# Front attention heads in pairs on the row halves of the array, constants set by DVE, and a new order of segments

## The chip, the cores and the metric

The kernel runs on one NeuronCore of a Trainium2 chip, as one launch. The metric is device time in microseconds (us): 547.35 us is the median of three runs (545.98 to 549.2).

The core has five instruction streams that run side by side and wait for one another through semaphores: PE (TensorE, the matrix engine; its weight loads are listed apart as PEld), DVE (VectorE), ACT (ScalarE), POOL (GpSimd) and SP (SyncE, which here issues every DMA). Each stream executes strictly in the order in which it was written. A place where one stream waits therefore holds up all that stands behind it in that stream.

## The reference

Eight sequences of 256 tokens by 128 features pass four layers, each with a layernorm ahead and a residual add behind:

```python
x = x + attn_a(layernorm(x))   # 16 heads of 8, rotary, causal over all 256 tokens
x = x + ffn(layernorm(x))      # gate, up, down; 352 wide
x = x + attn_b(layernorm(x))   # 16 heads of 8, RMS norm of q and k, causal in groups of 32 tokens
x = x + ffn(layernorm(x))      # the same weights again

def attn_a(x):
    q, k, v = heads(x @ Wq.T), heads(x @ Wk.T), heads(x @ Wv.T)
    q, k = q * cos + rotate(q) * sin, k * cos + rotate(k) * sin
    scores = einsum('bhqd,bhkd->bhqk', q, k) * 8 ** -0.5 + causal_mask
    return merge(softmax(scores) @ v) @ Wo.T

def fp4_linear(x, w):          # x and w are rounded to FP4 in blocks of 16 first
    return einsum('bsk,nk->bsn', fp4(x), fp4(w))

def ffn(x):
    return fp4_linear(silu(fp4_linear(x, w_gate)) * fp4_linear(x, w_up), w_down)
```

## The kernel before, in words

**Stages.** A batch is one sequence, held as two tiles of 128 tokens. Per batch there are four stages: front attention (`attn_a`), FFN a, local attention (`attn_b`), FFN b. Batches don't depend on one another; the stages of one batch do. Ahead of everything stand a setup (constants, masks, the attention weights transposed by PE) and the FP4 rounding of the FFN weights, a chain of wide operations on DVE called `weights` (L1162 to L1189), whose result PE transposes (L681 to L689).

**Front attention.** `front1` normalises the batch (moments on DVE, the root on POOL, the centring L1202 on DVE), transposes it, forms q, k and v on PE (L726, L729), applies the rotation (L1243, L1244) and splits q and k into three bf16 parts each, of which products are formed for nearly f32 accuracy. SP writes the parts to DRAM (`scatter`, L608) and reads them back stacked (`fetch`, L619): head by head 8 features by 6 part products, which is 48 rows. The even heads stand on partitions 0 to 47, the odd heads on 64 to 111. In `Kf` a pair of heads shares one column block, one head on each half. In `Qf` every head has a column block of its own, with the 64 rows of the other half zero, so that a matmul over all 128 rows adds nothing from the neighbour. `front2` makes the scores twice. First (L746 to L750) query by key, of which DVE takes each row's maximum (L1252); the negated maxima are split in three, transposed, and written by DMA into three further rows of `Qf` (`max_rows`, L626), where `Kf` has ones. Then (L765 to L769) key by query with the maximum subtracted, of which ACT takes the exponential (L963); PE multiplies by V (L780). V has a column of ones beside its 8 columns, which yields the softmax denominators. Since the three rows must be zero in the first pass, SP copies `zrows` into them ahead of each fetch (L639). The second pass goes round three PSUM banks (`ring`), so PE may start a pair only when the exponential of the first head of the pair before is done (L763).

**Local attention.** It has the same form, but `Ql` and `Kl` hold pairs on both halves and its matmuls address one half each (`rows`, L828; L847). The block of scores starts with a mask matmul over all 128 rows (L822, L845); the product with V (L858) uses 32 columns of the array at a time.

**Waits at the start.** PE and ACT go past the setup only when `ones_ready` is set, at the end of POOL's memsets (L1040 to L1056). DVE waits for the first DMAs and casts the masks (L1154 to L1160).

**Order.** `TIMES` gives every segment of every stage and batch a position for each engine, and `weave` writes each engine's stream in that order. `FFN_TURNS` fixes in what sequence the two FFNs use banks 6 and 7. Nothing is scheduled at run time.

Of the kernel before, what the change touches and what calls it, by code (L numbers as in the profile page):

```python
# [70 lines left out]
14  # L71
# [52 lines left out]
70 72 77
105 106 114
156 159 165
206 208 214
264 267 272
316 318 323
356 358 360  # L130
387 388 392""",
    "pe.local2": """
# [9 lines left out]
40 42 45 54 57 59 66
74 75 79 88 90 91 95
109 111 115 127 130 142 147
161 163 166 183 188 190 195
210 215 220 243 245 247 248
265 269 271 294 297 301 303
315 320 325 342 344 346 348
357 359 361 379 381 383 384""",
    "pe.ffn_b2": """  # L150
172 174 179 223 226 229 231
254 255 259 275 278 279 284
307 308 311 332 334 337 340
350 352 354 364 366 368 370
372 374 377 389 390 391 393
395 397 400 409 411 412 414
# [1206 lines left out]
```

## Time and profile before

| | |
|---|---|
| Median of three runs | 547.35 us (545.98 to 549.2) |
| The profiled execution | 545.92 us |
| its span, first to last instruction | 543.8 us |
| PE busy | 396.0 us, 73% of the span, 4061 matmuls |
| DVE busy | 356.7 us, 66% |
| ACT busy | 202.9 us, 37% |
| POOL busy | 176.3 us, 32% |
| Mean granted TensorE clock | 0.881 |
| Chain that ended last, by engine | PE 52%, DVE 22%, ACT 8%, DMA 6%, POOL 5% |

The profiled execution is 1.4 us below the median. 2.1 us of it lie outside the span. A matmul's busy time contains the way through the array, so that the busy times of neighbours overlap: the pace of PE is read from start to start, not from the mean duration of one. The granted clock is a share of full speed; 0.5 would be the lower of its two levels.

### The profile page before, as it was taken

Reading aid. Unit: us, or ns where it says so; the run is one execution under the profiler, and the core shown is the slowest. Engines: PE = TensorE matmul, PEld = TensorE weight load, DVE = VectorE, ACT = ScalarE, POOL = GpSimd, SP = SyncE. Lnnn points to the kernel's source line nnn. Section 1 sums busy time; section 2 is a strip of 40 time slices with the busy share of each in tenths; the row PEclk is TensorE's granted clock in tenths of the full one; section 3 lists DMA queues with packets and bytes.
Section 4 is the critical chain, followed back from the end, with each engine's and each line's share of the span. In section 5 each row is a group of like instructions: output and inputs, shape, how many; then the busy total and the mean of one; then the engine's idle time right before and its main releaser. Section 6 shows DMA issues by size and latency. Waiting matters only on the chain.

```text
span 543.8 us, 10363 instructions
## 1 busy us (share of the span) xinstructions
PE 396.0 (73%) x4061; PEld 254.1 (47%) x4061; DVE 356.7 (66%) x894; ACT 202.9 (37%) x548; POOL 176.3 (32%) x207
## 2 busy tenths in 40 slices
PE   0031777587686789979978989889996958769543
PEld 0021434455455446745755665565563544344312
DVE  2982704746754855977899988898779584542531
ACT  1001052171371067266347437536633613414100
POOL 9512031213333053153247333612542514210302
PEclk9999968888897889979989999998997997867755
DMA  7105050030163036026216313410400502400000
GB/s 226 36 0 118 1 120 2 23 97 2 31 149 59 3 99 138 3 61 143 36 34 149 70 31 93 107 21 7 117 13 17 111 2 65 64 14 0 5 6 10
DMA packets 59936, 31.03 MB, mean 57 GB/s; under 512 B 3248, under 2 KB 59504, under 8 KB 59888
## 3 DMA queue, kind: packets, MB, share of 16 engines
q1 hardware_dynamic: 59888, 30.37, 24.1%
q8 instruction: 32, 0.52, 0.4%
q14 instruction: 16, 0.13, 0.1%
HBM read 16.14 MB, written 13.63 MB: 55 GB/s over the span
## 4 chain that ended last, share of the span: by engine, by line
PE 52%; DVE 22%; ACT 8%; DMA 6%; POOL 5%; issue 3%; SPq 3%; POOLq 0%; ACTq 0%; DVEq 0%
PE bank L889 7%; DVE bmax L1252 6%; PE bank L726 4%; PE bank L904 4%; PE bank L850 4%; PE bank L858 4%; PE bank L845 3%; PE bank L694 3%; PE bank L765 3%; PE bank L780 3%; PE bank L897 2%; DMA Qf<-nmTf 2%; PE bank L705 2%; PE bank L807 2%; PE bank L748 2%
## 5 line engine op out<-in xcount | busy, mean ns | idle before, releaser
L1252 DVE TENSOR_REDUCE bmax<-bank 128x3 f32<-128x384 f32 x128 | 62.3, 550 | 13.8 <-PE bank L750 12.7
L963 ACT ACTIVATE prob<-bank 128x384 f32<-128x384 f32 x128 | 56.6, 494 | 23.0 <-PE bank L769 21.6
L1006 ACT ACTIVATE probl<-bank 128x512 f32<-128x512 f32 x64 | 38.2, 598 | 40.3 <-PE bank L850 39.6
L765 PE MATMUL bank<-Qf,Kf 128*128 128x256 bf16 x128 | 28.3, 308 | 24.0 <-DMA Qf<-nmTf 17.5
L1324 DVE SCALAR_TENSOR_TENSOR fb__hg<-fb__th,bank 128x352 f32<-128x352 f32 x16 | 8.3, 520 | 36.2 <-ACT fb__th L1024 35.9
L889 PE MATMUL bank<-wguT,fb__xqT 128*128 128x352 f32 x64 | 27.6, 561 | 3.2 <-DVE fb__h L1325 1.7
L780 PE MATMUL bank<-prob,Vf 128*32 128x128 f32 (+1 forms) x512 | 28.6, 342 | 1.8 <-ACT oTf L924 1.8
L845 PE MATMUL bank<-maskb,identb 128*128 128x512 bf16 x64 | 25.7, 401 | 5.6 <-ACT probl L1006 4.0
L924 ACT ACTIVATE xnTf<-bank 128x256 f32<-128x256 f32 x8 | 3.1, 384 | 71.5 <-PE bank L694 71.5
L1103 POOL TENSOR_TENSOR fb__w<-fb__w,fb__c 128x704 f32<-128x704 f32 x8 | 13.4, 1679 | 49.3 <-DVE fb__w L1214 49.3
L765 PEld LDWEIGHTS bank<-Qf,Kf 128*128 128x128 bf16 x128 | 9.2, 102 | 42.4 <-DMA Qf<-nmTf 19.4
L858 PE MATMUL bank<-probl,Vl 128*32 128x128 f32 x512 | 27.7, 289 | 1.0 <-ACT probl L1006 1.0
L769 PE MATMUL bank<-maskb,identb 128*128 128x256 bf16 x128 | 28.3, 308 | 0.0
L746 PE MATMUL bank<-Kf,Qf 128*128 128x128 bf16 x128 | 19.3, 236 | 11.7 <-DMA Kf<-scr_f 7.6
L748 PE MATMUL bank<-Kf,Qf 128*128 128x256 bf16 x128 | 27.0, 296 | 0.0
L750 PE MATMUL bank<-maskb,identb 128*128 128x256 bf16 x128 | 27.0, 296 | 0.0
L694 PE MATMUL bank<-identf,xnf 128*128 128x128 f32 x16 | 3.6, 309 | 31.7 <-DVE xnf L1202 24.7
L889 PE MATMUL bank<-wguT,fa__xqT 128*128 128x352 f32 x64 | 25.8, 533 | 0.7 <-ACT fa__xqT L924 0.6
L850 PE MATMUL bank<-Ql,Kl 51*128 51x128 bf16 x256 | 26.1, 224 | 0.0
L1078 POOL TENSOR_TENSOR qk<-ra,rb 128x512 f32<-128x512 f32 x8 | 10.7, 1337 | 45.6 <-DVE rb L1244 45.6
L850 PEld LDWEIGHTS bank<-Ql,Kl 51*128 51x128 bf16 x256 | 14.7, 96 | 20.7 <-issue 20.7
L726 PE MATMUL bank<-xnTf,wT 128*128 128x256 f32 x64 | 21.7, 498 | 3.2 <-ACT xnTf L924 3.2
(212 smaller groups left out, 996.2 us busy)
## 6 DMA issues: line engine op xcount, KB each, us to landing
scr_f<-partsf SPq DMA_DIRECT2D x16, 192.0 KB, 2.4
Qf<-scr_f SPq DMA_DIRECT2D x16, 192.0 KB
Kf<-scr_f SPq DMA_DIRECT2D x16, 192.0 KB
scr_l<-partsl SPq DMA_DIRECT2D x16, 192.0 KB, 3.3
Ql<-scr_l SPq DMA_DIRECT2D x16, 192.0 KB, 3.5
Kl<-scr_l SPq DMA_DIRECT2D x16, 192.0 KB, 4.8
scr_f<-partsf SPq DMA_DIRECT2D x16, 128.0 KB, 1.9
scr_l<-partsl SPq DMA_DIRECT2D x16, 128.0 KB, 2.6
```

The costliest lines, as they stand in the source:

```text
L726: mm = pe.matmul(bank[n // 2][:, (n % 2) * SEQ:(n % 2 + 1) * SEQ], wT[:, n, :], xnTf[:, :], start=True, stop=True)
L748: pe.matmul(ring4(2 * g + j)[:, 128:384], Qf[:, 2 * g + j, 128:256], Kf[:, g, 0:256], start=False, stop=True, skip_group_check=True)
L765: pe.matmul(ring(2 * g + j)[:, 0:256], Kf[:, g, 0:128], Qf[:, 2 * g + j, 0:256], start=True, stop=True)
L769: pe.matmul(ends(ring(2 * g + j)), identb[:, :], mask_kq, start=False, stop=True, skip_group_check=True).then_inc(f.s_st_ps, 1)
L780: mm = pe.matmul(bank[3][32 * j:32 * j + 32, k * P:SEQ], Vf[:, k, h, :], prob[:, h % 8, 256 * k:256 + 128 * k], start=(k == 0), stop=(k == ...
L845: pe.matmul(bank[4][:, :], identb[:, :], mask_blk, start=True, stop=True)
L850: mm = pe.matmul(bank[4][:, j * P:(j + 1) * P], Kl[r, g, k], Ql[r, g, k], start=False, stop=True, skip_group_check=True)
L858: mm = pe.matmul(bank[5][32 * j:32 * j + 32, t * P:(t + 1) * P], Vl[:, t, 2 * (4 * (G % 2) + j) + G // 2, :], probl[:, (u - 1) % 2, j, :], ...
L889: mm = pe.matmul(bank[6 + m][:, 0:I], w.xqT[:, t * P:(t + 1) * P], wguT[:, m, :], start=True, stop=True)
L963: act.activation(prob[:, h % 8, :], bank[h % 3][:, 0:384], ACT.Exp).then_inc(f.s_exp, 1)
L1006: act.activation(probl[:, u % 2, :, :].rearrange("p c n -> p (c n)"), bank[4][:, :], ACT.Exp).then_inc(l.s_exp, 1)
L1252: dve.tensor_reduce(bmax[:, h, :], bank[h % 4][:, 0:384].rearrange("p (n k) -> p n k", k=P), AX.X, ALU.max).then_inc(bmax_done, 1)
```

## The change

1. `Qf` becomes 8 column blocks, like `Kf` and `Ql`: two heads in one block, on the two halves. Each score matmul of the front addresses one half (48 rows in the first pass, 51 in the second). The first pass no longer reads the three rows of the maxima, so `zrows` and its DMA go, and PE waits for 64 instead of 96 counts.
2. POOL keeps four small memsets. The ones in K and V and the zeros in the maxima's tiles are set by DVE, between its memset of `fw` and its wait for the first DMAs. V is filled with ones throughout: its unused columns then yield denominators that nobody reads. `Qf` needs no memset.
3. `TIMES` and `FFN_TURNS` are replaced.

```diff
-        Qfs = [sb(f"Qf{i}", [P, H, SEQ], BF16) for i in range(2)]
+        Qfs = [sb(f"Qf{i}", [P, PAIRS, SEQ], BF16) for i in range(2)]
...
 # SP, front1
-                for r in range(2):
-                    sp.dma_start(side(Qfs[b % 2], 64 * r + NSTACK, 3, r), zrows[:, :]).then_inc(f.s_stack[b % 2], 16)
                 fetch(b, f, scr_f, Qfs[b % 2], Kfs[b % 2])
...
 # PE, front2
+                side = [slice(64 * r, 64 * r + NSTACK) for r in range(2)]
+                shifted = [slice(64 * r, 64 * r + KROWS) for r in range(2)]
...
-                        pe.wait_ge(f.s_stack[b % 2], (b // 2 + 1) * 96)
+                        pe.wait_ge(f.s_stack[b % 2], (b // 2 + 1) * 64)
...
-                        pe.matmul(ring4(2 * g + j)[:, 0:128], Qf[:, 2 * g + j, 0:128], Kf[:, g, 0:128], start=True, stop=True)
+                        pe.matmul(ring4(2 * g + j)[:, 0:128], Qf[side[j], g, 0:128], Kf[side[j], g, 0:128], start=True, stop=True)
...
-                            pe.matmul(ring(2 * g + j)[:, 0:256], Kf[:, g, 0:128], Qf[:, 2 * g + j, 0:256], start=True, stop=True)
+                            pe.matmul(ring(2 * g + j)[:, 0:256], Kf[shifted[j], g, 0:128], Qf[shifted[j], g, 0:256], start=True, stop=True)
...
 # POOL
-            for n, tile in enumerate((Vf, *Vls)):
-                pool.memset(tile[:, :, :, :], 0.0).then_inc(pool_chain, 1)
-                pool.wait_ge(pool_chain, n + 1)
-                pool.memset(tile[:, :, :, HD:HD + 1], 1.0)
-            for tile in Kfs:
-                pool.memset(tile[:, :, :], 1.0)
-            for tile in Qfs:
-                pool.memset(tile[:, :, :], 0.0)
-            pool.memset(zrows[:, :], 0.0)
-            pool.memset(Kls[0][:, :, :], 1.0)
-            pool.memset(Kls[1][:, :, :], 1.0).then_inc(ones_ready, 1)
...
 # DVE
             dve.memset(fw[:, :], 0.0).then_inc(fw_zero, 1)
+            for tile in (*Kfs, *Kls):
+                dve.memset(tile[:, :, :], 1.0)
+            for tile in (Vf, *Vls):
+                dve.memset(tile[:, :, :, :], 1.0)
+            for tile in (npartf, npartl):
+                ins = dve.memset(tile[:, :, :], 0.0)
+            ins.then_inc(ones_ready, 1)
             dve.wait_ge(w_loaded, 80)
...
 # TIMES
     "pe.weights": """
-2""",
+4""",
...
     "dve.weights": """
-1 2 3 4 5 6 7 8 10 11 12 15 16""",
+1 3 4 5 8 9 10 11 12 14 15 16 17""",
     "dve.front1": """
-0 9 13
-14 17 35
+0 2 6
+7 13 35
```

What the new positions do to the streams is shown at three places. Line numbers are those of the kernel that a piece belongs to.

DVE, start of the program behind the setup, before (`stf` and `mvf` are the moments of a front batch, `xnf` its centred values; `fw`, `fs`, `fu`, `fa` and `fg` belong to the FFN weights):

```order
L1193 BN_STATS stf<-xall 128x6 x2
L1196 BN_AGGR mvf<-stf 128x2 x2
L1166 TENSOR_REDUCE fs<-fw 128x70
L1167 TENSOR_SCALAR fs<-fs 128x70
L1168 RECIPROCAL fs<-fs 128x70
L1170 TENSOR_TENSOR fu<-fw,fs 128x1120
L1172 SCALAR_TENSOR_TENSOR fa<-fu 128x1120
L1175 TENSOR_SCALAR fg<-fa 128x1120
L1178 SCALAR_TENSOR_TENSOR fg<-fa,fg 128x1120 x2
L1180 TENSOR_SCALAR fg<-fg 128x1120
L1183 SCALAR_TENSOR_TENSOR fg<-fa,fg 128x1120
L1202 TENSOR_SCALAR xnf<-xall,mvf,rsf 128x128 x2
```

The centring of batch 0 stands behind ten operations of `weights`. In the changed kernel, the same place (`ra` and `rb` are the rotation of batch 0):

```order
L1184 BN_STATS stf<-xall 128x6 x2
L1187 BN_AGGR mvf<-stf 128x2 x2
L1157 TENSOR_REDUCE fs<-fw 128x70
L1158 TENSOR_SCALAR fs<-fs 128x70
L1159 RECIPROCAL fs<-fs 128x70
L1193 TENSOR_SCALAR xnf<-xall,mvf,rsf 128x128 x2
L1161 TENSOR_TENSOR fu<-fw,fs 128x1120
L1163 SCALAR_TENSOR_TENSOR fa<-fu 128x1120
L1166 TENSOR_SCALAR fg<-fa 128x1120
L1234 TENSOR_TENSOR ra<-bank,ropet 128x512
L1235 TENSOR_TENSOR rb<-bank,ropet 128x512
```

The centring of batch 0 now stands behind three operations of `weights`, and the rotation behind three more.

PE, the same part of the program, before (`fw` rows: transposes of the rounded FFN weights; `Kf,Qf` and the mask behind it: a pair of heads of the first pass):

```order
L694 MATMUL bank<-identf,xnf 128x128 x2
L726 MATMUL bank<-xnTf,wT 128x256 x4
L729 MATMUL bank<-wT,xnTf 128x128 x2
L686 MATMUL bank<-identf,fw 128x128 x4
L686 MATMUL bank<-identf,fw 128x96 x2
L688 MATMUL bank<-identf,fw 128x128 x2
L688 MATMUL bank<-identf,fw 96x128
L746 MATMUL bank<-Kf,Qf 128x128 x2
L748 MATMUL bank<-Kf,Qf 128x256 x2
L750 MATMUL bank<-maskb,identb 128x2x128 x2
```

The transposes of the FFN weights stand ahead of the first pair. In the changed kernel:

```order
L688 MATMUL bank<-identf,xnf 128x128 x2
L720 MATMUL bank<-xnTf,wT 128x256 x4
L723 MATMUL bank<-wT,xnTf 128x128 x2
L742 MATMUL bank<-Kf,Qf 128x128 x2
L744 MATMUL bank<-Kf,Qf 128x256 x2
L746 MATMUL bank<-maskb,identb 128x2x128 x2
L742 MATMUL bank<-Kf,Qf 128x128 x2
L744 MATMUL bank<-Kf,Qf 128x256 x2
L746 MATMUL bank<-maskb,identb 128x2x128 x2
L680 MATMUL bank<-identf,fw 128x128 x4
L680 MATMUL bank<-identf,fw 128x96 x2
L682 MATMUL bank<-identf,fw 128x128 x2
```

They now stand behind the second pair.

PE, around the first local scores (`Kl,Ql`, with the mask `maskb` of 512 columns ahead), before (`oTf` and `attnf`: the end of front batch 2; `fa__` and `fb__`: FFN a and b):

```order
L780 MATMUL bank<-prob,Vf 32x256 x4
L780 MATMUL bank<-prob,Vf 32x128 x4
L705 MATMUL bank<-identf,oTf 128x128 x8
L822 MATMUL bank<-maskb,identb 128x512 x2
L829 MATMUL bank<-Kl,Ql 32x32 x128
L694 MATMUL bank<-identf,attnf 128x128 x2
L897 MATMUL bank<-identf,fa__u 128x128 x2
L897 MATMUL bank<-identf,fa__u 96x128
L792 MATMUL bank<-wT,attnTf 128x128 x2
L904 MATMUL bank<-wdT,fa__hqT 128x128 x3
```

The local scores stand ahead of the last steps of front batch 2. In the changed kernel:

```order
L742 MATMUL bank<-Kf,Qf 128x128 x2
L744 MATMUL bank<-Kf,Qf 128x256 x2
L746 MATMUL bank<-maskb,identb 128x2x128 x2
L742 MATMUL bank<-Kf,Qf 128x128 x2
L744 MATMUL bank<-Kf,Qf 128x256 x2
L746 MATMUL bank<-maskb,identb 128x2x128 x2
L818 MATMUL bank<-maskb,identb 128x512 x2
L825 MATMUL bank<-Kl,Ql 32x32 x128
L742 MATMUL bank<-Kf,Qf 128x128 x2
```

They now stand behind the first five pairs of front batch 3 (two of them shown), and so behind the whole of front batch 2.

## Rows read from the trace of the kernel before

**Rows 1.** Timeline of the setup on DVE: start us, us, engine, line, operation, tiles, [idle before].

```profile
1.04 0.99 DVE L1153 MEMSET fw<- 128x1120 f32 x1 [1.04 <-PEq L1352]
...
11.04 1.03 DVE L1156 CAST maskb<-fa 128x512 bf16<-128x512 f32 x1 [9.01 <-DMA lnw<-in_L_attn_b_ln_w_dram]
...
11.99 4.07 DVE L1157 CAST maskb<-fu 128x1024 bf16<-128x1024 f32 x1
...
15.98 3.90 DVE L1158 TENSOR_SCALAR lnw<-lnw 128x128 f32<-128x128 f32 x1
...
19.98 0.23 DVE L1160 TENSOR_SCALAR lnw<-lnw 128x128 f32<-128x128 f32 x1
```

**Rows 2.** Timeline of the same stretch on POOL.

```profile
8.27 7.25 POOL L1053 MEMSET Qf<- 128x4096 bf16 x2
...
18.00 1.79 POOL L1056 MEMSET Kl<- 128x2048 bf16 x1
```

**Rows 3.** Timeline on DVE from the first moments to the FFN weights' end.

```profile
20.13 0.48 DVE L1193 BATCH_NORM_STATS2 stf<-xall 128x6 f32<-128x128 f32 x2
...
20.81 1.29 DVE L1166 TENSOR_REDUCE fs<-fw 128x70 f32<-128x1120 f32 x1
...
25.70 0.74 DVE L1175 TENSOR_SCALAR fg<-fa 128x1120 f32<-128x1120 f32 x1
...
26.48 2.69 DVE L1178 SCALAR_TENSOR_TENSOR fg<-fa,fg 128x1120 f32<-128x1120 f32 x2
...
31.34 0.60 DVE L1202 TENSOR_SCALAR xnf<-xall,mvf,rsf 128x128 f32<-128x128 f32 x2
...
37.18 0.69 DVE L1243 TENSOR_TENSOR ra<-bank,ropet 128x512 f32<-128x512 f32 x1 [1.28 <-PE bank L726]
...
42.11 2.16 DVE L1188 TENSOR_TENSOR fw<-fu,fs 128x1120 f32<-128x1120 f32 x1
```

**Rows 4.** Timeline of batch 0's way to its scores, on SP, PE and DVE.

```profile
41.58 4.53 SPq L614 DMA_DIRECT2D scr_f<-partsf  x6
...
44.32 1.44 PE L686 MATMUL bank<-identf,fw 128*128 128x128 f32 x6 [6.40 <-DVE fw L1188]
...
46.16 1.68 SPq L639 DMA_DIRECT2D Qf<-zrows  x2
...
54.05 0.40 PE L746 MATMUL bank<-Kf,Qf 128*128 128x128 bf16 x2 [7.64 <-DMA Kf<-scr_f]
...
55.12 8.12 DVE L1252 TENSOR_REDUCE bmax<-bank 128x3 f32<-128x384 f32 x16 [8.25 <-PE bank L750]
```

**Rows 5.** DMA issues: tiles, queue, count, KB each, median us from issue to landing.

```profile
scr_f<-partsf SPq DMA_DIRECT2D x16, 64.0 KB, 1.6
```

**Rows 6.** Busy time by stretch: us, busy us of PE, PEld, DVE, ACT, POOL; granted clock, DMA.

```profile
0.00:54.00 54.00, 8.49 (x27) 6.28 (x27) 32.95 (x36) 5.75 (x16) 26.25 (x31) 1.00 0.35 95
...
240.00:400.00 160.00, 146.34 (x1735) 95.36 (x1728) 132.90 (x353) 87.56 (x241) 63.54 (x74) 0.98 0.32 72
...
480.00:544.00 64.00, 35.83 (x199) 20.54 (x199) 23.88 (x61) 12.20 (x30) 9.70 (x10) 0.63 0.02 7
```

**Rows 7.** Timeline on PE in front attention's second half.

```profile
159.06 0.39 PE L765 MATMUL bank<-Qf,Kf 128*128 128x256 bf16 x2
...
160.26 0.39 PE L765 MATMUL bank<-Qf,Kf 128*128 128x256 bf16 x2 [0.47 <-ACT prob L963]
...
160.60 0.38 PE L769 MATMUL bank<-maskb,identb 128*128 128x256 bf16 x2
```

**Rows 8.** Timeline on PE in local attention, where full-height and half-height operations alternate.

```profile
422.73 0.39 PE L845 MATMUL bank<-maskb,identb 128*128 128x512 bf16 x1 [0.69 <-ACT probl L1006]
...
423.05 0.39 PE L850 MATMUL bank<-Ql,Kl 51*128 51x128 bf16 x4
...
423.37 0.43 PE L858 MATMUL bank<-probl,Vl 128*32 128x128 f32 x8
```

**Rows 9.** Timeline on PE at batch 0's local scores.

```profile
169.06 1.03 PE L822 MATMUL bank<-maskb,identb 128*128 128x512 bf16 x2 [4.26 <-DMA Kl<-scr_l]
```

More of the change, by code:

```diff
@@ L70 @@
 8
-14
+13
 19
@@ L79 @@
 23 24
-29 30
+29 31
 36 37
-41 42
+40 42
 45 46
-49 51""",
+49 50""",
     "sp.local2": """
-13
+14
 21
-27
+28
 35
-40
-44
+39
+43
 48
@@ L94 @@
     "sp.store": """
-31
-38
-43
+30
+41
+44
 47
-50
+51
 53
@@ L108 @@
 35 36
-65 67
-102 103
-148 149
+65 66
+101 102
+145 146
 199 200
-249 251""",
+246 248""",
     "pe.front2": """
[1 row of a table removed]
[1 row of a table added]
 27 28 29 30 31 32 33 34 37 38 39 41 43 44 46 47 48 49 50 51 52 53
[5 rows of a table removed]
-286 287 289 291 292 296 298 299 306 310 312 314 317 319 321 322 324 327 328 330 336 339""",
-    "pe.local1": """
[L124 to L131, printed above, removed]
-    "pe.local2": """
[7 rows of a table removed]
-410 413 415 416 418 420 421 423 424 425 426 427 428 429""",
-    "pe.ffn_a2": """
[L142 to L149, printed above, removed]
-    "pe.ffn_b2": """
[L151 to L156, printed above, removed]
[5 rows of a table added]
+284 285 287 289 291 293 294 297 299 302 305 307 309 310 312 314 317 319 320 322 325 327""",
+    "pe.local1": """
+76 80 84
+109 111 117
+159 162 168
+214 216 223
+266 268 272
+313 316 323
+352 354 358
+386 388 389""",
+    "pe.local2": """
[7 rows of a table added]
+409 411 415 416 418 420 421 423 424 425 426 427 428 429""",
+    "pe.ffn_a2": """
+40 42 45 54 57 58 69
+71 73 77 86 88 90 93
+104 105 113 131 135 139 148
+151 155 161 175 178 181 186
+195 196 203 228 234 238 251
+253 256 260 275 277 279 300
+303 308 315 338 340 342 344
+346 348 350 366 368 369 371""",
+    "pe.ffn_b2": """
+165 167 171 212 218 219 224
+264 267 270 318 321 324 326
+329 331 335 353 355 356 357
+359 360 363 375 377 378 380
+382 384 387 392 394 395 397
+399 401 404 410 412 413 414
 417 419 422 430 431 432 433
@@ L218 @@
 9 12 14 15
-16 21 22 24
-26 32 33 36
-37 43 44 47
-48 56 57 59
-60 70 71 73""",
+16 20 22 24
+25 33 34 35
+36 43 44 46
+47 57 58 60
+61 70 71 73""",
     "pool.front2": """
@@ L233 @@
     "pool.local1": """
-20 25 27
-31 35 38
-42 49 51
-55 61 64
-69 76 79
-83 85 88
+23 26 29
+32 37 39
+45 50 53
+56 64 67
+72 75 79
+83 85 87
 92 94 96
-100 102 104""",
+99 102 104""",
     "pool.ffn_a1": """
 11 13
-19 23
-30 34
-41 46
-54 58
-68 72
+19 21
+30 31
+41 42
+54 55
+68 69
 81 82
-90 91""",
+89 90""",
     "pool.ffn_a2": """
 18
-29
-39
-53
-67
-80
-89
-98""",
+27
+40
+51
+62
+76
+86
+95""",
     "pool.ffn_b1": """
-45 50
-62 66
-74 75
-84 86
+48 49
+63 66
+74 77
+84 88
 93 97
-99 103
+100 101
 106 107
@@ L269 @@
     "pool.ffn_b2": """
-63
-77
-87
-95
-101
+59
+80
+91
+98
+103
 105
@@ L278 @@
     "dve.weights": """
[L279 removed]
+1 3 4 5 8 9 10 11 12 14 15 16 17""",
     "dve.front1": """
[L281 to L282 removed]
+0 2 6
+7 13 35
 36 37 60
[L284 to L288 removed]
+61 64 91
+92 99 133
+134 137 169
+170 177 221
+222 229 263""",
     "dve.front2": """
@@ L292 @@
 72 73 74 75 76 77 78 79 80 81 82 83 84 85 86 87 89 106 108
[4 rows of a table removed]
[L297 to L314 removed]
[4 rows of a table added]
+288 289 290 291 292 293 294 295 296 297 299 300 301 302 303 304 306 327 330""",
+    "dve.local1": """
+96 97 104 105
+132 135 138 142
+173 176 185 188
+209 213 233 237
+266 269 280 283
+312 315 324 328
+343 346 355 359
+367 368 382 384""",
+    "dve.local2": """
+131 168 172
+175 220 225
+227 264 267
+271 310 313
+316 341 344
+348 369 372
+374 390 392
 395 406 407""",
@@ L317 @@
 40 57 59 62
-71 91 96 97
-110 129 134 135
-147 169 174 176
-191 197 216 221
-240 250 263 268
-289 297 305 313
-337 339 341 342""",
-    "dve.ffn_a2": """
-63 65 66 67 68 88 90
-99 102 103 104 105 109 124
-138 140 141 142 143 145 165
-182 184 185 187 188 202 212
-230 233 235 237 239 257 262
-279 281 283 285 287 304 312
-328 330 331 332 334 340 344
-357 361 362 363 365 371 374""",
-    "dve.ffn_b1": """
-175 177 178 180
-223 228 231 232
-270 273 275 277
-316 321 323 325
-347 352 354 360
-375 380 381 383
-394 396 398 400
+71 88 90 93
+109 120 127 129
+146 155 164 166
+195 199 201 203
+241 256 259 261
+298 305 307 309
+331 332 334 335""",
+    "dve.ffn_a2": """
+63 65 66 67 68 94 95
+98 100 101 102 103 107 130
+136 139 140 141 143 167 171
+178 181 183 184 186 194 207
+218 224 226 228 230 262 265
+270 272 274 276 278 308 311
+318 321 322 323 326 339 342
+347 349 351 354 357 364 366""",
+    "dve.ffn_b1": """
+174 179 180 182
+231 232 235 239
+268 273 275 279
+314 317 319 320
+345 350 352 358
+373 376 377 379
+394 396 398 399
 408 409 411 413""",
     "dve.ffn_b2": """
-189 192 222 224 226 236 247
-269 272 274 276 278 286 290
-318 320 322 324 326 335 338
-349 351 353 355 358 364 366
-367 368 370 372 379 384 386
-387 388 389 390 391 397 399
+187 189 191 192 223 234 238
+277 281 282 285 287 325 329
+333 336 337 338 340 353 356
+360 361 362 363 365 370 371
+375 378 380 381 383 385 386
+387 388 389 391 393 397 400
 401 402 403 404 405 410 412
@@ L614, in scatter @@
                         sp.dma_start(scr[m][:, products, :], src).then_inc(a.s_wrote, 16)
-            def side(tile, row, n, r):
-                return tile[row:row + n, r:H:2, :] if any(tile is q for q in Qfs) else tile[row:row + n, :, :]
             def fetch(b, a, scr, Q, K):
```

99 lines of the change are left out of this document (38 added, 61 removed), and 70 rows, old and new, of tables (FFN_TURNS, TIMES).

## The prediction, made before the changed kernel had run

> **What bounds the kernel now.** I read the table of the page first: PE is busy for 73% of the span and holds 52% of the chain that ended last. Then the busy time by stretch [rows 6]. The reader is to see three parts. In the first 54 us PE works for 8.5 us: the start is a chain of latencies. From 240 to 400 us PE is busy for 146 of 160 us at a granted clock of 0.98, almost its upper level: here PE is near its limit. From 480 us on PE is busy for little more than half of the time at a clock of 0.63, in a chain of dependent steps that the edits of the array don't enter. Then the timelines of the start [rows 1 to 4], which show who waits there, and those of the operations that change [rows 7, 8].
>
> **The setup on DVE and POOL.** DVE waits 9.01 us for its DMAs, until 11.04, and then needs until 20.13 for five small operations [rows 1, 3]. The reader is to see that 128 elements take 3.90 us in one of them and 0.23 us in the last [rows 1], and that POOL's memsets end at 19.79, just ahead of the fast one [rows 2]. I read this as DVE held up by POOL's writes. POOL keeps some 256 elements, so this goes.
> - Added on DVE: memsets of 4 x 2048 + 3 x 1024 + 2 x 256 = 11,776 elements. At 0.99 us for 1120 [rows 1] this is 10.4 us; POOL's 1.79 for 2048 [rows 2] gives 10.3. From 2.03 on they end at 12.4. They lie inside the wait up to 11.04, so 1.4 us come out. Bounds: 0.74 us for 1120, a tensor_scalar [rows 3], gives 7.8 us, hidden wholly (11.04); 1.29 for 1120, the slowest reading of them [rows 3], gives 13.6 us (15.6). I take 12.4, since it is from memsets.
> - The five operations, undisturbed: 128 elements take 0.23 and 1120 take 0.74 [rows 1, 3], a slope of 0.51 ns. 512, 1024 and three times 128 elements then take 0.43 + 0.69 + 0.69 = 1.8 us.
> - So the moments of batch 0 start at 14.2 (12.8 to 17.4 by the bounds) instead of 20.13.
>
> The Trainium skill, "VectorE: DVE Perf Modes", section on zero memsets, says a memset takes one cycle per element whatever the type; at the 0.96 GHz of the same page that is an estimate of 12.3 us, and the start would be 14.3 + 1.8 = 16.1. The row of 0.99 us is faster than that rule; the sum goes by the row.
>
> **Batch 0 to its scores.** Before, the centring starts at 31.34, since ten operations of the weights stand ahead of it. Now three do. Moments take 20.81 - 20.13 = 0.68. The three operations take 25.70 - 20.81 less two wide ones of 1.35, so 2.2 [rows 3]. The centring starts at 14.2 + 0.7 + 2.2 = 17.1. The rotation followed it by 37.18 - 31.34 = 5.84 [rows 3]; DVE's own work between them, 0.6 + 2.7 + 0.74, fits in. It starts at 22.9, 14.3 us earlier. The scores followed by 54.05 - 37.18 = 16.9 [rows 3, 4]: they start at 39.8.
>
> The two issues of the zero rows take 1.68 us on SP [rows 4]. They start 0.05 after the scatter's last issue ends, and the fetch behind them must await the landing of that scatter, 1.6 us [rows 5]. So they are hidden, and their going gains 0.1. For later batches I count nothing either; the bound is 1.7 us a batch where the fetch is late.
>
> **The FFN weights become late.** The cover that the weights had is gone: they now run behind the rotation, which ends at 24.3. What is left: moments of batch 1 0.7, six wide operations 8.1, two of 0.74, a centring 0.6, two last ones of 2.16 [rows 3]: 15.2 us, so 39.5, and up to 1 more if the centring waits for POOL's root, which stands behind the third part. PE reaches their transposes after two pairs. The maxima pace the pairs at 8.12 / 8 = 1.02 us [rows 4], so that is at 41.8: no wait. But the transposes themselves, 1.44 us for six and so 2.2 for nine [rows 4], now stand between pairs. DVE has four heads' maxima done at 42.9 and gets the next at 45.1: it loses 2.2. The maxima of batch 0 end at 39.8 + 9.2 + 2.2 = 51.2 instead of 63.24. **12.0 us earlier.** All that follows is held by this batch's maxima and exponentials, not by loads, so I carry the 12.0 to the end.
>
> **The array.** A pair's four score matmuls, 768 columns, take 160.60 - 160.26 = 0.34 us [rows 7], 0.44 ns a column. If the halves overlap this is 0.17. Against that stands the change between full height (the mask) and half height. In local attention 512 columns of mask are followed after 0.32 us by the half-height ones, and 512 columns of these again after 0.32 by the next form [rows 8], where 0.44 ns a column is 0.23: 0.09 per change. So a pair with both changes needs 0.17 + 0.18 = 0.35 against 0.34, no gain where PE is the limit: +1.3 us over 128 pairs. In the second pass the exponential waits for the pair: 1.20 us from pair to pair [rows 7]; from idle the first change may cost nothing, and the mask starts up to 0.08 earlier, in 7 x 8 steps up to 4.5 us. I take half of that: -0.9 in all. The bounds: halves that don't overlap, +0.18 x 128 = +23; free changes, -0.17 x 128 = -22.
>
> The rule of the Trainium skill that speaks against the change is in "TensorEngine Tiling (Array Packing)", key properties: to change the tiling mode drains the engine. It agrees with the 0.09 us of [rows 8]. The same page promises up to 2x; by that alone the sum would have 22 us more.
>
> **The order elsewhere.** Before, PE waits 4.26 us for the local operands at batch 0's local scores [rows 9], and the last steps of front batch 2 stand behind them. Now these steps and five pairs of front batch 3 go first. Front batch 3 gains up to 4.3 us; the local scores lose up to 5 pairs, 5.1 us, less the 4.3. I take -2 (from -4.3 to +0.8). The positions of the last 100 rows or so on PE are nearly alike, so the tail stays.
>
> **Sum.** The profiled execution took 545.92: span 543.8 and 2.1 around it. 545.92 - 12.0 - 0.9 - 2.0 = 531.0. The median of the runs lies 1.4 above it: **532.5 us**.
>
> **Rivals.**
> - The packing pays in full. For: half the columns' time goes. Against: [rows 8]. In the first pass DVE's maxima set the pace (1.02 us a pair [rows 4]), so it pays in the 64 pairs of the second: -10.9 instead of -0.9, 522.5 us.
> - Slower: the changes of height aren't paid back, because the second half's matmul waits for the first. Place: all 128 pairs, between 100 and 400 us, where PE is the limit [rows 6]. Price: 0.18 us each, +23: 556 us. It decides from 0.12 us a pair on (15 us of gain over 128). Against: the pairs of the first pass have slack under DVE's 1.02.
> - The gain is given back. The local stage and FFN b end the program; if their chain, whose first step is now behind five pairs, falls back by some 5 us at this and at one or two later batches, 12 us are gone: 545 us. For: the rest of the order was set for other durations. Against: PE's last rows stand where they stood.
> - The five operations on DVE are slow by themselves. Then they take 9.1 us behind 12.4, the moments start at 21.5, and of the 12.0 us 4.7 are left: 540 us. Against: 3.90 beside 0.23 us for 128 elements.
>
> **How the numbers follow.** Forecast 0.58, packing in full 0.12, slower 0.10, given back 0.13, slow operations 0.07. The forecast's own range is 527 to 538 (memsets -1.4 to +3.2, local scores -2.3 to +2.8, array -3.6 to +2.2). The whole range takes in the first and, nearly, the third rival: 521 to 546. About 0.5%, 2.7 us, is what can be told from no change: faster means below 544.6. Forecast, packing, slow operations and a third of the given back make 0.82; the rest of that case 0.08; slower 0.10.
>
> **What would show it.** Setup: the casts on DVE at 0.4 and 0.7 us, moments at about 14, first scores at about 40, the FFN transposes behind the second pair without a wait, the last maximum of batch 0 at about 51. Array: in the second pass a pair's mask 0.25 to 0.35 us after its start; PE's busy time nearly unchanged. Order: no wait at the first local scores. I am wrong if the two halves start their matmuls more than half a matmul apart, if the lead of 12 us at batch 0's maxima isn't there, or if it is there and shrinks by batch 7.

## The result and the profile after

| | before | changed |
|---|---|---|
| Median of 20 runs each, side by side | 547.21 us | 549.85 us |
| Ratio, 95% interval | | 1.0077 [1.0049, 1.0105] |
| Profiled execution, its span | 545.92, 543.8 us | 548.96, 547.2 us |
| PE, DVE, ACT, POOL busy | 396.0, 356.7, 202.9, 176.3 us | 398.5, 349.8, 204.0, 158.7 us |
| Mean granted clock | 0.881 | 0.832 |

The ratio is of fast runs alone: it leaves out three of the changed kernel's 20 executions (555.6 to 563.6 us), in a slower state, which the median includes.

The changed kernel is 0.8% slower. The forecast was 532.5 us, so both the sign and the range (521 to 546) were wrong.

The start came out nearly as forecast. DVE's timeline of the changed kernel (start, duration, engine, line, operation; idle time before in brackets), which answers to [rows 1, 3]:

```profile
1.04 0.99 DVE L1137 MEMSET fw<- 128x1120 f32 x1 [1.04 <-PEq L1343]
2.41 1.76 DVE L1139 MEMSET Kf<- 128x2048 bf16 x1 [0.38 <-issue]
4.55 1.76 DVE L1139 MEMSET Kf<- 128x2048 bf16 x1 [0.38 <-issue]
...
14.01 0.36 DVE L1147 CAST maskb<-fa 128x512 bf16<-128x512 f32 x1
14.29 0.68 DVE L1148 CAST maskb<-fu 128x1024 bf16<-128x1024 f32 x1
...
15.42 0.48 DVE L1184 BATCH_NORM_STATS2 stf<-xall 128x6 f32<-128x128 f32 x2
...
18.28 0.60 DVE L1193 TENSOR_SCALAR xnf<-xall,mvf,rsf 128x128 f32<-128x128 f32 x2
...
24.11 0.69 DVE L1234 TENSOR_TENSOR ra<-bank,ropet 128x512 f32<-128x512 f32 x1 [1.86 <-PE bank L720]
...
46.27 5.66 DVE L1243 TENSOR_REDUCE bmax<-bank 128x3 f32<-128x384 f32 x12 [1.35 <-PE bank L746]
```

The reader is to see the casts at 0.36 and 0.68 us (forecast 0.4 and 0.7), the moments at 15.4 (14.2), the rotation at 24.1 (22.9), and the last maximum ending at 46.27 + 5.66 = 51.9 (51.2) instead of 63.2. The lead over before is 11.3 us. PE in the same stretch, which answers to [rows 4]:

```profile
42.06 0.29 PE L742 MATMUL bank<-Kf,Qf 48*128 48x128 bf16 x2 [17.20 <-DMA Kf<-scr_f]
...
43.87 1.38 PE L680 MATMUL bank<-identf,fw 128*128 128x128 f32 x6
```

The transposes of the FFN weights come behind the second pair and wait for nothing, as forecast. The second pass of a later batch, at the upper level of the clock, which answers to [rows 7]:

```profile
183.45 0.28 PE L761 MATMUL bank<-Qf,Kf 51*128 51x256 bf16 x2 [1.26 <-DMA Qf<-nmTf]
...
183.72 0.39 PE L765 MATMUL bank<-maskb,identb 128*128 128x256 bf16 x2
184.58 0.28 PE L761 MATMUL bank<-Qf,Kf 51*128 51x256 bf16 x2 [0.47 <-ACT prob L959]
```

The mask stands 0.27 us behind the pair's start instead of 0.34, and from pair to pair it takes 1.13 us instead of 1.20. So the halves overlap, and a pair gains 0.07 us. Still the lead does not reach the end. The busy time by stretch of the changed kernel (busy us of PE, PEld, DVE, ACT, POOL, then granted clock, DMA share, GB/s; the last two rows answer to [rows 6]):

```profile
54.00:100.00 46.00, 32.91 (x203) 15.14 (x201) 18.55 (x54) 12.35 (x29) 7.77 (x10) 0.61 0.17 36
100.00:150.00 50.00, 38.91 (x298) 21.10 (x298) 27.82 (x73) 20.74 (x51) 15.83 (x20) 0.80 0.24 57
...
240.00:400.00 160.00, 140.27 (x1702) 82.86 (x1702) 124.50 (x348) 81.23 (x215) 59.14 (x73) 0.96 0.27 63
480.00:547.20 67.20, 39.44 (x325) 22.97 (x324) 25.82 (x67) 12.75 (x32) 13.61 (x14) 0.60 0.02 7
```

and of before:

```profile
54.00:100.00 46.00, 32.42 (x241) 19.68 (x241) 22.18 (x59) 11.46 (x27) 6.07 (x8) 0.85 0.16 36
```

Two things are to be seen. From 54 to 100 us PE is granted 0.61 instead of 0.85. And from 240 to 400 us it is busy for 140 us instead of 146, so it stands idle for 20 us instead of 14.

The starts of some steps in both traces (us) show where the lead goes. For FFN b it is its first step on DVE (`fb__hg`), for the last steps of front and local attention the residual add on DVE:

| | before | changed | lead |
|---|---|---|---|
| last maximum of batch 0 (end) | 63.2 | 51.9 | 11.3 |
| first scores of batch 1 | 90.1 | 82.8 | 7.3 |
| last front step of batch 7 | 395.7 | 380.3 | 15.4 |
| FFN b of batch 2 | 369.1 | 386.0 | -16.9 |
| last local step of batch 7 | 508.5 | 511.9 | -3.4 |
| FFN b of batch 7 | 521.8 | 525.2 | -3.4 |

### The profile page after: what moved, and what is told of

It is laid out like the page before. It is cut to its first block, busy times and chain, and to the rows that moved or that the text cites. A ratio compares the mean times of both kernels' runs of the same rounds, so it can differ in the third digit from the quotient of the medians.

```text
span 547.2 us, 10351 instructions
## 1 busy us (share of the span) xinstructions
PE 398.5 (73%) x4061; PEld 225.7 (41%) x4061; DVE 349.8 (64%) x903; ACT 204.0 (37%) x548; POOL 158.7 (29%) x192
## 4 chain that ended last, share of the span: by engine, by line
PE 52%; DVE 22%; ACT 8%; POOL 6%; DMA 6%; issue 4%; SPq 2%; POOLq 0%; ACTq 0%; DVEq 0%
PE bank L885 7%; DVE bmax L1243 5%; PE bank L720 4%; PE bank L900 4%; PE bank L846 4%; PE bank L854 3%; PE bank L841 3%; DMA Qf<-nmTf 3%; PE bank L765 3%; PE bank L776 3%; PE bank L688 2%; PE bank L746 2%; PE bank L761 2%; PE bank L893 2%; PE bank L825 2%
## 5 line engine op out<-in xcount | busy, mean ns | idle before, releaser
L959 ACT ACTIVATE prob<-bank 128x384 f32<-128x384 f32 x128 | 56.7, 493 | 25.4 <-PE bank L765 24.1
L761 PE MATMUL bank<-Qf,Kf 51*128 51x256 bf16 x128 | 20.3, 313 | 23.7 <-DMA Qf<-nmTf 16.1
L776 PE MATMUL bank<-prob,Vf 128*32 128x128 f32 (+1 forms) x512 | 30.0, 356 | 4.1 <-ACT oTf L920 3.9
L885 PE MATMUL bank<-wguT,fb__xqT 128*128 128x352 f32 x64 | 29.4, 591 | 5.0 <-DVE fb__h L1316 3.8
L742 PE MATMUL bank<-Kf,Qf 48*128 48x128 bf16 x128 | 15.5, 239 | 20.8 <-DMA Kf<-scr_f 17.2
L765 PE MATMUL bank<-maskb,identb 128*128 128x256 bf16 x128 | 29.4, 317 | 0.3 <-issue 0.3
L1324 DVE TENSOR_TENSOR xall<-bank,xall 128x128 f32<-128x128 f32 x32 | 9.1, 286 | 31.0 <-PE bank L900 30.8
L746 PE MATMUL bank<-maskb,identb 128*128 128x256 bf16 x128 | 28.4, 308 | 0.0
L720 PE MATMUL bank<-xnTf,wT 128*128 128x256 f32 x64 | 24.2, 544 | 3.5 <-ACT xnTf L920 3.4
L846 PEld LDWEIGHTS bank<-Ql,Kl 51*128 51x128 bf16 x256 | 15.4, 99 | 22.8 <-issue 22.8
L761 PEld LDWEIGHTS bank<-Qf,Kf 51*128 51x128 bf16 x128 | 6.4, 95 | 44.4 <-DMA Qf<-nmTf 17.9
L885 PE MATMUL bank<-wguT,fa__xqT 128*128 128x352 f32 x64 | 23.8, 498 | 1.1 <-ACT fa__xqT L920 1.1
L900 PE MATMUL bank<-wdT,fb__hqT 128*128 128x128 f32 (+1 forms) x96 | 19.5, 355 | 4.7 <-ACT fb__hqT L920 3.4
```

Of the source, the lines that this page charges most:

```text
L720: mm = pe.matmul(bank[n // 2][:, (n % 2) * SEQ:(n % 2 + 1) * SEQ], wT[:, n, :], xnTf[:, :], start=True, stop=True)
L746: pe.matmul(ends(ring4(2 * g + j)), identb[:, :], mask_qk, start=False, stop=True, skip_group_check=True).then_inc(f.s_sc_ps, 1)
L765: pe.matmul(ends(ring(2 * g + j)), identb[:, :], mask_kq, start=False, stop=True, skip_group_check=True).then_inc(f.s_st_ps, 1)
L776: mm = pe.matmul(bank[3][32 * j:32 * j + 32, k * P:SEQ], Vf[:, k, h, :], prob[:, h % 8, 256 * k:256 + 128 * k], start=(k == 0), stop=(k == ...
L846: mm = pe.matmul(bank[4][:, j * P:(j + 1) * P], Kl[r, g, k], Ql[r, g, k], start=False, stop=True, skip_group_check=True)
L885: mm = pe.matmul(bank[6 + m][:, 0:I], w.xqT[:, t * P:(t + 1) * P], wguT[:, m, :], start=True, stop=True)
```

## The experiments

Each run is given by its ratio to the kernel before, which ran beside it on the same chip, with a 95% interval. One per cent is 5.5 us; the intervals are some 0.3 to 0.7% to either side, so differences between two runs below about 0.7% are not told apart.

**One part at a time (e1 to e4).** e1 is the changed kernel with the old `TIMES` and `FFN_TURNS`; e2 is e1 with the new positions of the start alone:

```diff
     "pe.weights": """
-2""",
+4""",
     "pe.front2": """
-3 4 5 6 7 ...
+2 3 5 6 7 ...
     "dve.weights": """
-1 2 3 4 5 6 7 8 10 11 12 15 16""",
+1 3 4 5 8 9 10 11 12 14 15 16 17""",
     "dve.front1": """
-0 9 13
-14 17 35
+0 2 6
+7 13 35
```

The line of `pe.front2` is marked short; only its first two positions change. e3 is before with the pairs on halves alone (the memsets of `Qf` and `zrows` go, POOL sets the other constants), e4 before with the new order alone.

> The changed kernel with TIMES and FFN_TURNS of the kernel before; pairs on the halves and constants on DVE stay. Theory 'the order': the new order gives the lead of the start back (the front runs 15 us ahead at batch 7, local attention and FFN b fall behind). Then the old order keeps what the setup gains: moments of batch 0 start at about 15.4 instead of 20.1, so -4.7 us, and 0 to -4 us for the array (a pair's mask starts 0.27 instead of 0.34 us after the pair): 539 to 543 us, ratio about 0.988. Rival 'the array': half-height matmuls cost later, through a lower granted clock (0.832 against 0.881 in the two profiles). Then this kernel shows the low clock too and is at 547 to 552 us, ratio 1.00 or above.

> As e1_old_order, but with the positions that the new order gives to the FFN weights and to the front's first stage of batches 0 and 1 on DVE, and to the transposes of the weights on PE (behind the first pair, not ahead). All else is the old order. Theory 'the order': the start's lead of 11 to 12 us at the maxima of batch 0 (as in the changed kernel) reaches the end, since nothing behind it is reordered: 532 to 537 us, ratio about 0.975. Rival 'the start is worth nothing, the middle has slack that eats it': lead at batch 0 of 11 us, but 545 us or above. Rival 'the array': as e1, 547 us or above.

> The kernel before with the pairs on the halves alone: old order, the constants of K and V still set by POOL (only the memsets of Qf and of the zero rows go, 8.0 us, so POOL's memsets end at about 11.8 instead of 19.8, and DVE's five small operations behind its DMAs are held up less). Theory 'the order': moments of batch 0 at about 13 to 14, so -6 us, array 0 to -4: 537 to 542 us. Rival 'the array': the clock falls to about 0.83 and the time is 547 us or above in spite of the 6 us.

> The kernel before with the new TIMES and FFN_TURNS alone; full height with zero rows, constants on POOL. Theory 'the order': the lead of the start is smaller (about 9 us at the first scores, since DVE's setup still ends at 20.1) and the tail is given back as in the changed kernel, local attention and FFN b late: 549 to 556 us, ratio 1.005 to 1.015. Rival 'the array': the order is good by itself, the start's 8 us come through: 537 to 541 us, clock near 0.88.

Measured: e1 1.0033 [1.0004, 1.0063], e2 0.9854 [0.9805, 0.9903], e3 1.0002 [0.9969, 1.0035], e4 0.9952 [0.991, 0.9993]. e1 and e3 were expected at 539 to 543 and 537 to 542 us if the order alone were at fault; both came out where the rival, a cost of the halves, had them. e4 was expected at 549 to 556 us and had a median of 542.8: the new order alone doesn't make the kernel slower. (Its one trace is of an execution of 882.1 us and is not read here.) The order of the start is worth 1.8% (e1 to e2), and the setup on DVE by itself nothing (e3 to e1), although the last maximum of batch 0 ends 6 us earlier in e1 (57.3) than before (63.2). The first scores of batch 1 start at 90.0 there, before at 90.1: the 6 us go in between, with the clock at 0.54 from 54 to 100 us. And from e2 to the changed kernel 2.2% are lost to the rest of the order.

That the constants needn't move to DVE for an early start is seen in e3. There POOL still sets them and its memsets end at 11.8 us, since those of `Qf` are gone, and DVE's moments start earlier than in the changed kernel (15.4):

```profile
12.61 0.21 DVE L1151 TENSOR_SCALAR lnw<-lnw 128x128 f32<-128x128 f32 x1
...
13.13 0.48 DVE L1186 BATCH_NORM_STATS2 stf<-xall 128x6 f32<-128x128 f32 x2
```

Its last maximum of batch 0 ends at 55.1. No run joins this setup with the new order of the start.

**The height of the matmuls (e5, e7, e8, e9, e12, e15).** e5 is e2 with full-height score matmuls as before, `Qf` with zero rows again, set by POOL while DVE sets the constants of K and V:

```diff
-pe.matmul(ring4(2 * g + j)[:, 0:128], Qf[side[j], g, 0:128], Kf[side[j], g, 0:128], ...)
+pe.matmul(ring4(2 * g + j)[:, 0:128], Qf[:, 2 * g + j, 0:128], Kf[:, g, 0:128], ...)
...
+for tile in Qfs:
+    pool.memset(tile[:, :, :], 0.0)
+pool.memset(zrows[:, :], 0.0).then_inc(ones_ready, 1)
```

e7 has halves only in the first pass (48 rows), e8 only in the second (51). e9 is e5 with the changed kernel's whole order. e12 has this order up to step 151 of PE, 177 of DVE, 149 of ACT, 49 of POOL and 17 of SP, and before's from there on. e10 and e15 (one kernel, run twice) are e12 on halves.

> As e2_new_start, but the front's score matmuls go over the full height again, with zero rows (DVE still sets the constants of K and V; POOL sets only the zeros of Qf and the zero rows, and is done ahead of DVE). In e1, e3 and the changed kernel the granted clock from 54 to 100 us was 0.54 to 0.61 against 0.85 before, and the lead over the kernel before shrank by 5 us between batch 0's maxima and batch 1's first scores. Theory 'the halves cost clock': here that clock is back at 0.85 or so, e2's lead of 13.9 us at the first scores is still there at batch 1's, and the time is 5 to 8 us below e2: 530 to 534 us, ratio about 0.973. Rival 'the lead shrinks there whatever the form, since batch 0 has slack behind its maxima': the same 538 to 540 us as e2, the same lead of 9 us at batch 1.

> As e5_full_height, but the first pass (the maxima) addresses one half per head; the second pass stays at full height. Theory 'the halves cost clock': the first pass is paced by DVE, so the cost shows as a clock that is still low when the second pass of batch 0 begins: between e5 and e2, about 535 us. Rival 'what costs is the change of height in the second pass, which ACT waits for': as e5.

> As e5_full_height, but the second pass (the exponentials) addresses one half per head; the first pass stays at full height. Theory 'the halves cost clock': the clock rises in the first pass of batch 0 as before (at 0.98 of full from there) and falls in the second: between e5 and e2, about 535 us. Rival 'only the change of height costs': as e2, 539 us. If the pairs' mask started 0.07 us earlier and nothing else changed, 7 x 8 x 0.07 = 4 us less than e5.

> The changed kernel, all of the new order kept, with the front's score matmuls at full height again (setup as in e5_full_height). Theory 'both parts cost, one by one': the halves cost here what they cost between e5 and e2 (8 us), the new order behind the start what it costs between e2 and the changed kernel (10 us): 538 to 542 us, ratio about 0.989, clock 0.86 or above. Rival 'the halves are the whole loss': as e5, 531 us. Rival 'the new order is the whole loss': as the changed kernel, 548 us.

> As e10_new_until_151, at full height with zero rows (setup as in e5_full_height). If halves and order add up, this is e10 less 8 us, 525 to 531 us, and no slower than e5's 530.8. If the new order's first 200 us cost, it is slower than e5: 535 us or more.

> Half-height matmuls with the new order for the first 150 steps or so and the order of before behind them, once more, since its first runs scattered from 531 to 554 us. If the order of these first steps costs nothing at half height either, as at full height, it takes 539 as the kernel with only a new start does (ratio 0.985). If it takes 543 to 546, the half-height matmuls make the new order of the middle dearer than it is at full height.

| order | full height | halves | the halves cost |
|---|---|---|---|
| before's, new start | e5 0.9734 [0.969, 0.9778] | e2 0.9854 [0.9805, 0.9903] | 1.2% |
| new up to step 151 | e12 0.9757 [0.9707, 0.9807] | e15 0.9937 [0.9901, 0.9972] | 1.8% |
| all new | e9 0.9895 [0.9828, 0.9963] | changed 1.0077 [1.0049, 1.0105] | 1.8% |

e7 gave 0.987 [0.9815, 0.9925], e8 0.9892 [0.985, 0.9934]: with halves in either pass the kernel is slower than e5. Both were expected between e5 and e2 and are not; halves in one pass cost as much as in both, as far as the intervals tell. Why they don't add up is not shown. e10, expected at 533 to 539 us, gave a median of 543.0 us over runs from 531 to 554 and no usable ratio; e15 repeats it. Down the columns the table prices the order: from step 151 on it costs 1.4% at either height, and up to there nothing that can be told at full height (0.2%) and 0.8% on halves.

The mean granted clock goes with the height in all of these kernels, not only in the traces. Over the executions that the ratios are made of it is 0.870 to 0.875 at full height (e5, e9, e12, e13; before 0.867 to 0.873), 0.827 to 0.838 on halves in both passes (changed, e1, e2, e3, e14, e15), 0.849 and 0.843 on halves in one (e7, e8), and with the added matmuls described below 0.868 (e6) and 0.851 (e11).

Where the halves lose is best seen in e12 and e15, which differ in nothing else but the setup and the reloading of the zeros that full height needs. e12:

```profile
54.00:100.00 46.00, 30.13 (x228) 18.68 (x232) 18.05 (x55) 16.50 (x40) 11.80 (x15) 0.81 0.22 52
100.00:150.00 50.00, 37.40 (x333) 25.83 (x326) 34.62 (x89) 22.79 (x64) 17.98 (x20) 0.93 0.26 60
150.00:200.00 50.00, 41.57 (x506) 27.26 (x505) 36.06 (x100) 21.59 (x60) 15.26 (x20) 0.97 0.41 89
```

and e15:

```profile
54.00:100.00 46.00, 33.08 (x202) 15.14 (x200) 18.56 (x54) 12.34 (x29) 7.95 (x10) 0.60 0.16 36
100.00:150.00 50.00, 38.80 (x286) 20.99 (x290) 27.23 (x72) 20.11 (x50) 15.67 (x20) 0.80 0.24 55
150.00:200.00 50.00, 38.70 (x435) 20.98 (x433) 34.82 (x92) 22.16 (x69) 16.06 (x20) 0.86 0.37 83
```

e15's first scores of batch 0 start 1.0 us later than e12's (41.5 and 40.5), those of batch 1 6.3 later, those of batch 3 10.5 later and those of batch 4 13.6 later (204.7 and 191.1); those of batch 7 are 11.8 later, and the two executions end 14.1 apart. (The ratios put the difference at 1.8%, 9.8 us; these two executions are further apart than the medians.) So nearly the whole loss arises in the first 205 us, where up to 200 us the granted clock is 0.60 to 0.86 instead of 0.81 to 0.97. It isn't the halves' own time, for where both are at the lower level the halves are the quicker ones. Batch 0's second pass in e12 (full height):

```profile
59.13 0.61 PE L765 MATMUL bank<-Qf,Kf 128*128 128x256 bf16 x2 [0.37 <-ACT prob L963]
...
60.74 0.61 PE L765 MATMUL bank<-Qf,Kf 128*128 128x256 bf16 x2 [0.37 <-ACT prob L963]
```

1.61 us from pair to pair; in e15 (halves):

```profile
62.25 0.40 PE L761 MATMUL bank<-Qf,Kf 51*128 51x256 bf16 x2 [0.37 <-ACT prob L959]
...
63.66 0.40 PE L761 MATMUL bank<-Qf,Kf 51*128 51x256 bf16 x2 [0.37 <-ACT prob L959]
```

1.41 us. What differs is that the clock rises at full height and stays low on halves. e5 at full height in batch 0's second pass, the last microseconds before its clock rises at 65.4, and then ten microseconds with it:

```profile
61.00:65.00 4.00, 3.51 (x27) 1.89 (x28) 0.60 (x2) 2.19 (x6) 1.44 (x3) 0.50 0.37 105
65.00:75.00 10.00, 6.98 (x90) 4.08 (x82) 0.86 (x4) 5.02 (x12) 0.73 (x1) 0.98 0.50 79
```

and e2 on halves, where it stays at 0.50:

```profile
61.00:65.00 4.00, 3.26 (x22) 0.87 (x22) 0.60 (x2) 2.89 (x8) 2.02 (x3) 0.50 0.35 98
65.00:75.00 10.00, 8.67 (x80) 3.08 (x76) 0.00 (x0) 5.02 (x12) 0.00 (x0) 0.50 0.45 79
```

The rows at one level are the ones to compare, for at the lower level every matmul lasts longer and the busy share is higher for the same work: 8.67 us for 80 matmuls in e2, 6.98 for 90 in e5. At that level PE was busy for 88% of the time in e5 ahead of the rise, and for 87% of ten microseconds in e2 without one. From pair to pair the halves do leave PE a little more idle, 0.37 of 1.41 us against 0.37 of 1.61.

**More work (e6, e11).** Into the kernels with halves goes one matmul of full height and 384 columns behind every pair of batches 0 and 1, in both passes, 32 in all, whose result nobody reads: e6 on e2, e11 on the changed kernel.

```diff
+if b < 2:
+    pe.matmul(bank[4][:, 0:384], identb[:, :], maskb[:, 512:896], start=True, stop=True)
```

> As e2_new_start with its half-height pairs, plus one full-height matmul of 384 columns that nobody reads (into bank 4, unused so far) behind every pair of both passes of batches 0 and 1: 32 more matmuls, PE work of 0.16 us each at the upper clock and 0.32 at the lower. Theory 'the halves cost clock': the added work raises the granted clock of 45 to 100 us, and in spite of it the lead at batch 1's scores is larger than e2's 9 us: 533 to 537 us. Rival 'the clock follows from other things, or what costs is the change of height itself': the work is only added, 32 x 0.16 to 0.32 us, of which what DVE or ACT don't hide comes out: 539 to 546 us.

> The changed kernel unchanged in its order and halves, plus e6's filler: one full-height matmul of 384 columns that nobody reads behind every pair of both passes of batches 0 and 1 (32 in all). Theory 'the halves cost clock': as between e2 and e6 some 3 us are regained although work is added: 543 to 547 us, granted clock from 54 to 100 us up from 0.61 to 0.8 or so. Rival 'e6's gain hung on e2's order': 548 to 554 us.

Measured: e6 0.9811 [0.977, 0.9852] beside e2's 0.9854; e11 0.9969 [0.993, 1.0008] beside the changed kernel's 1.0077. The first difference, 0.4%, is too small to be told from none; the second, 1.1% or 5.9 us, is clear: more work makes this kernel faster. e11 from 54 to 100 us:

```profile
54.00:100.00 46.00, 32.83 (x244) 16.56 (x243) 18.47 (x54) 15.21 (x36) 9.92 (x13) 0.80 0.19 45
```

The clock is 0.80 instead of 0.61, and in the same time PE does 244 matmuls instead of 203 (19 of them added ones). Its batch 3 begins its scores at 156.4 us, the changed kernel's at 161.4. In this execution, which took 549.93 us and so 4.9 above its median, that lead is gone by batch 7 (340.8 and 339.2), so that the gain rests on the ratio alone. The added matmuls can help only by what they do to the clock. They give back some 0.6 of what the halves cost in the new order (1.1 of 1.8%); in e6, where the mean clock is back at 0.868, it is 0.4 of 1.2%, inside the noise. They also close PE's idle time between the pairs, so they don't tell whether it is the half height that keeps the clock low or the fewer columns and longer gaps that come with it.

**What in the later order costs (e13, e14).** In both kernels with the whole new order PE waits 6.3 us for `qkn` of batch 7. e13 (on e9) and e14 (on the changed kernel) move two steps ahead of the FFN's rounding:

```diff
     "dve.local1": """
-367 368 382 384""",
+367 368 379.5 384""",
     "pool.local1": """
-99 102 104""",
+99 100.5 104""",
```

> Full height and the whole new order, with two steps of local attention of batch 7 moved ahead: on DVE the scaling of q and k (qkn) goes ahead of the rounding of FFN b of batch 4 (6 operations, 3.45 us), on POOL the root for it goes ahead of that FFN's finish of batch 5. In the kernel without this PE waits 6.35 us for qkn, and 0.6 at this place in the kernel before. If this wait is a piece of what the order behind the start loses, PE waits some 3 us there and local attention of batches 6 and 7 ends some 3 us earlier: time 537 (ratio 0.983 instead of 0.9895). If the wait only stands in for another one (POOL's long finish of the FFN's rounding comes 1.1 us later then, and FFN b of batch 4 with it), the lead is gone again by the scores of batch 7 and the time stays at 540.

> The changed kernel with the same two steps moved ahead. The wait of 6.34 us on qkn becomes some 3, the time some 3 us less than the changed kernel's: ratio 1.002 instead of 1.0077, if the wait is a piece of the loss; 1.0077 if it only stands in for another.

Measured: e13 0.9833 [0.9778, 0.9888], e14 1.003 [0.9992, 1.0067]: the numbers expected if this wait were a piece of the loss, but the intervals overlap those of e9 and the changed kernel, and the trace contradicts it. PE in e9:

```profile
435.97 1.45 PE L807 MATMUL bank<-wqkvb,xnTl 128*128 128x384 f32 x4
443.77 1.12 PE L694 MATMUL bank<-identf,qkn 128*128 128x128 f32 x4 [6.35 <-DVE qkn L1277]
446.39 0.58 PE L845 MATMUL bank<-maskb,identb 128*128 128x512 bf16 x1 [1.50 <-DVE restl L1283]
```

and in e13:

```profile
433.67 1.45 PE L807 MATMUL bank<-wqkvb,xnTl 128*128 128x384 f32 x4
438.88 0.66 PE L694 MATMUL bank<-identf,qkn 128*128 128x128 f32 x4 [3.75 <-DVE qkn L1277]
444.02 0.58 PE L845 MATMUL bank<-maskb,identb 128*128 128x512 bf16 x1 [4.49 <-DVE restl L1283]
```

The wait went down by 2.6 us and the next one up by 3.0, since `restl` still stands behind that rounding on DVE. From L807 to L845 it takes 10.4 us in both. The 2.4 us by which e13 is earlier here were there ahead of the moved steps. So the trace gives no gain to this wait, and it isn't shown to be what the order loses.

What the traces show of the loss is a balance. e9 and e12 have the same order up to about 150 us. e9 is already 3.4 us behind there (first scores of batch 3 at 154.9 and 151.5), which the order can't have done. Then e9 finishes the front stage of batch 7 at 371.3 us, e12 at 376.5; but its last local step of batch 1 is 8.4 us late, its FFN b of batch 2 26.6. From the end of the front stages to the end of the program, e9:

```profile
371.30:537.70 166.40, 115.18 (x1099) 66.78 (x1097) 83.12 (x219) 50.21 (x134) 43.47 (x48) 0.75 0.15 33
```

and e12:

```profile
376.50:528.00 151.50, 106.43 (x1006) 60.90 (x1005) 79.48 (x206) 44.02 (x119) 37.00 (x43) 0.73 0.12 28
```

93 matmuls more are left over for the last stretch, where PE is busy for 70% at a clock of 0.75. It is 14.9 us longer, against 5.2 us gained ahead of it: 9.7 us, of which 3.4 were there before the orders part. The ratios make it 1.4%, 7.6 us. The changed kernel and before read alike: 166.5 us against 147.7 behind the front stages, 1099 matmuls against 1007.

## Why the prediction was wrong

**Setup and start, "12.0 us earlier": right.** 11.3 us were measured. The memsets took 1.6 us more than I gave them, since I took the duration in a row for the pace: the row of `Kf` says 1.76 us for 2048 elements, the next one starts after 2.14, which is 1.04 ns per element. The rule that I had set aside, one cycle per element ("VectorE: DVE Perf Modes", the section on zero memsets, of the Trainium skill), gave 14.3 for their end; they ended at 14.0. The moments came 1.2 us late for that, the first scores 2.3. The rival that the five operations are slow by themselves is out: they took 1.4 us. The lead does reach the end where nothing takes it back: e5, at full height and with only the start reordered, takes 0.9734, 14.5 us less than before.

**"All that follows is held by this batch's maxima and exponentials": wrong for the changed kernel.** It leaves out that PE's speed isn't given. Of the lead of 11.3 us at batch 0's maxima 7.3 were left at batch 1's first scores, at a clock of 0.61 instead of 0.85.

**The array, "-0.9 in all" with bounds of +23 and -22: the failed step, the first of two.** The working for one clock held: the halves start 3 ns apart (median of 64 pairs in either pass), the mask 0.27 us behind the pair's start (forecast 0.25 to 0.35), and a pair gains 0.07 us. The step priced columns and changes of height, and took the clock of the traced kernel for the changed one's. The halves cost 1.2% to 1.8%, 7 to 10 us, by the pairs of kernels in the table. These are inside the bounds of the array, but the bounds were for halves that don't overlap, and these do. In the changed kernel 1.1 of the 1.8% come back with added full-height work and a clock of 0.80 instead of 0.61. Why the chip grants less to halves is not shown. "TensorE: Matmul & The Clock Gate" of the Trainium skill (section "What's actually happening") says that the clock follows how busy PE has been. The busy time that the rows record doesn't decide it here: at the lower level 3.51 of 4 us came ahead of a rise in e5, and 8.67 of 10 us of none in e2. Whether the height counts, the columns or the gaps, no run separates.

**The order elsewhere, "-2" and "the tail stays": the failed step, the second.** It costs 1.4%, 7.6 us, from step 151 on. I read that PE's last hundred rows stood nearly alike and concluded that their time would too. But rows that stand alike can begin with more work undone ahead of them. The wait at batch 0's local scores, which I took to be gone, is still 2.96 us:

```profile
168.54 1.04 PE L818 MATMUL bank<-maskb,identb 128*128 128x512 bf16 x2 [2.96 <-DMA Kl<-scr_l]
```

The rival "the gain is given back" named the right place, the chain of local stages and FFN b, with a chance of 0.13; its price of 12 us was above the 7.6 that the order behind step 151 costs by itself. The rival "slower" had the right sign for the wrong cause: the change ahead of the mask cost 0.10 us (0.27 less the 0.17 of overlapping columns, forecast 0.09), and the overlap paid for it where the clock was the same.

**Sum.** Full height with the new start (e5) -2.7%; the order up to step 151 (e12) +0.2; from there on (e9) +1.4; the halves (changed) +1.8. These are the steps from one measured kernel to the next, so that they end at the measured 0.8% by themselves and prove nothing by their sum; the halves' 1.2% with before's order shows that the prices depend on the order, or on the noise. The best version is e5 (0.9734), the change without its halves and without its later order; e12 can't be told from it.

**What stays open.** Which of the moves behind step 151 costs, and whether it is `FFN_TURNS` or `TIMES`; moving the one wait that was tried showed no gain that can be told, and an order that switches at a later step wasn't tried. What the added matmuls don't give back of the cost of the halves is not traced either: they stood in batches 0 and 1 alone and take time themselves.

## What to carry to other kernels

Ahead of packing half-height matmuls, ask what the granted clock is in that stretch and whether full-height work keeps it up: columns saved on an array that then runs at its lower level are no gain, and a trial with a few useless full-height matmuls can tell it. Here it did in one order (1.1%) and not in the other (0.4%); the same pairs at full height told it in both. A lead at the front of a pipeline is only worth what the last stretch gets of it: compare how much work is left when the first stage ends, not how the last rows stand. And a change of three parts is to be taken apart; here the start alone was worth 2.7%, and the other two gave all of it back.
